# Causal attention stage: one of three products of denominator and reciprocal on GpSimd instead of VectorE

## What is computed

```python
x = x + attn_a(layernorm(x))
x = x + ffn(layernorm(x))          # two layers: local attention, then gated feed-forward
x = x + attn_b(layernorm(x))
x = x + ffn(layernorm(x))
```

```python
dot = einsum('bhid,bhjd->bhij', q, k)
vals = q_norm_sq + k_norm_sq.transpose(0, 1, 3, 2)
scores = dot * dot / (vals - 2.0 * dot + EPSILON)
attn = softmax(scores + mask)      # mask: triu(k=1) * -1e9
out = einsum('bhij,bhjd->bhid', attn, v)
```

## Time and profile before

| | us |
|---|---|
| median of 3 runs | 4480.62 |
| lowest and highest | 4475.3, 4484.98 |
| the profiled execution's span | 4472.0 |
| of that, stage b (from about 1960 to 3080) | 1120 |
| PE, DVE, ACT, POOL busy over the whole span | 93%, 74%, 57%, 37% |

### The profile page before, as it was taken

The page is one execution under the profiler, slowest core; times in us unless marked ns, Lnnn a source line. Parts: engine busy times, 40 slices in busy tenths (PEclk is TensorE's granted clock), DMA queues, the critical chain, the costliest instruction groups (busy, mean ns, idle before and its releaser), DMA issues.

```text
span 4472.0 us, 65596 instructions
## 1 busy us (share of the span) xinstructions
PE 4154.4 (93%) x23120; PEld 2610.2 (58%) x23120; DVE 3296.2 (74%) x7689; ACT 2542.1 (57%) x5480; POOL 1674.2 (37%) x1816
## 2 busy tenths in 40 slices
PE   8999989999999999988888888888999999999997
PEld 4665556666666666554555555555565665665664
DVE  5667777777667767659999999988677777677663
ACT  4555554445444445449888888876554444454441
POOL 2222355445546555330010001013464464455451
PEclk9999999999999999998888888788999999999999
DMA  2000000000000000000000001101000000100000
GB/s 78 10 16 6 24 10 5 3 3 5 23 22 18 13 8 10 23 21 18 22 20 22 20 18 28 34 20 29 9 6 3 3 25 8 30 20 17 13 19 22
DMA packets 63093, 78.57 MB, mean 18 GB/s; under 512 B 15344, under 2 KB 47392, under 8 KB 62768
## 3 DMA queue, kind: packets, MB, share of 16 engines
q1 hardware_dynamic: 62768, 74.39, 5.9%
HBM read 36.63 MB, written 12.58 MB: 11 GB/s over the span
## 4 chain that ended last, share of the span: by engine, by line
PE 64%; DVE 21%; issue 6%; ACT 5%; POOL 2%; DMA 0%; SPq 0%; POOLq 0%; DVEq 0%; ACTq 0%
PE wide L865 44%; PE o_ps L865 8%; PE wide L868 7%; PE turn_ps L868 5%; DVE x L1287 3%; DVE turned L1338 2%; DVE w_up L1387 2%; PE turn_ps L865 2%; DVE prob L1410 1%; DVE w_up L1381 1%; DVE prob L1399 1%; POOL prob L1603 1%; DVE x L1393 1%; ACT prob L1243 1%; DVE turned L1341 1%
## 5 line engine op out<-in xcount | busy, mean ns | idle before, releaser
L865 PE MATMUL wide<-x,w_up 128*128 128x512 f32 (+3 forms) x2528 | 853.8, 554 | 3.8 <-DVE x L1491 2.4
L865 PE MATMUL wide<-w_in,x_t 128*128 128x512 f32 (+2 forms) x1920 | 811.8, 567 | 17.5 <-ACT q_t L1164 8.1
L1603 POOL TENSOR_SCALAR prob<-prob,st 128x256 f32<-128x256 f32 (+1 forms) x1024 | 501.4, 508 | 775.9 <-DVE st L1423 773.6
L1223 ACT ACTIVATE prob<-prob,st 128x256 f32<-128x256 f32 (+1 forms) x1024 | 479.2, 471 | 249.1 <-DVE st L1410 248.7
L865 PEld LDWEIGHTS wide<-w_in,x_t 128*128 128x128 f32 x1920 | 341.4, 192 | 368.5 <-issue 359.6
L865 PEld LDWEIGHTS wide<-x,w_up 128*128 128x128 f32 (+2 forms) x2528 | 374.7, 198 | 288.5 <-issue 274.9
L865 PE MATMUL o_ps<-pt,v 128*32 128x128 f32 (+2 forms) x5120 | 509.3, 345 | 16.8 <-DVE pt L1439 8.6
L1576 POOL TENSOR_TENSOR sines<-raw,rot 128x512 f32<-128x512 f32 x256 | 354.0, 1403 | 331.3 <-ACT raw L1152 331.1
L865 PEld LDWEIGHTS o_ps<-pt,v 128*64 128x64 f32 (+1 forms) x5120 | 326.3, 133 | 236.6 <-issue 154.0
L1584 POOL TENSOR_TENSOR rn<-ss,minus_half 128x16 f32<-128x16 f32 x128 | 423.8, 3311 | 105.5 <-DVE ss L1333 98.7
L1254 ACT ACTIVATE o_t<-o_ps 128x512 f32<-128x512 f32 x192 | 114.2, 595 | 508.0 <-PE o_ps L865 508.0
(11 more groups left out here) (161 smaller groups left out, 7476.4 us busy)
## 6 DMA issues: line engine op xcount, KB each, us to landing
kept<-resid SPq DMA_DIRECT2D x16, 512.0 KB, 3.0
x<-kept SPq DMA_DIRECT2D x16, 512.0 KB, 3.3
w_up<-hid SPq DMA_DIRECT2D x62, 128.0 KB, 2.2
x<-hid SPq DMA_DIRECT2D x62, 128.0 KB, 2.4
shifted<-resid SPq DMA_DIRECT2D x32, 224.0 KB
w_in<-in_f_wqkv SPq DMA_DIRECT2D x4, 1536.0 KB, 6.4
w_up<-in_f_w SPq DMA_DIRECT2D x4, 1492.0 KB, 6.5
resid<-in_x SPq DMA_DIRECT2D x8, 512.0 KB, 9.0
```

What stands on the lines that cost most here:

```text
L865: return eng.matmul(out, lhsT, rhs, start=start, stop=stop, skip_group_check=True)
L1223: last = eng.activation(pr[:, local_span(t)], pr[:, local_span(t)], ACT.Exp, bias=sm[:, t:t + 1], scale=-1.0, accum_out=sm[:, 4 + t:5 + t])
L1603: last = eng.tensor_scalar(pr[:, local_span(t)], pr[:, local_span(t)], sm[:, 8 + t:9 + t], 1.0, ALU.mult, ALU.mult)
```

## The change

In steps with k % 3 == 2 the part `bclose` is replaced by a part `pclose`, which makes the same product on POOL. There are eight such steps in each of the eight units, 64 in all. The other 128 stay on DVE. `bmul` waits for whichever of the two its step has. In the planner `pclose` costs 2.5 us, where `bclose` at this width costs 0.1 + 0.277 * 4 = 1.21 us.

```diff
-        "DVE": "... bss bclip bclose bmul low inv ...",
-        "POOL": "rstd_h sin rn brow bias_b ...",
+        "POOL": "rstd_h sin rn brow pclose bias_b ...",
...
+    if kind == "pclose":
+        return 2.5
...
+def close_kind(k):
+
+    return "pclose" if k % 3 == 2 else "bclose"
...
-            put("bclose", k, at + 1 / steps, final("bguess", k))
-            put("bmul", k, at + 1.5 / steps, final("bclose", k), final("bnum", k), *scaled)
+            put(close_kind(k), k, at + 1 / steps, final("bguess", k))
+            put("bmul", k, at + 1.5 / steps, final(close_kind(k), k), final("bnum", k), *scaled)
...
-                    dve.wait_ge(S["bclose"], o)
+                    dve.wait_ge(S[close_kind(i)], nth(close_kind(i), u, i))
...
+                elif kind == "pclose":
+                    den, inv = close_home(u, i)
+                    pool.wait_ge(S["bguess"], nth("bguess", u, i))
+                    eng.tensor_tensor(den, den, inv, ALU.mult).then_inc(S["pclose"], 1)
```

More of the change, by code:

```diff
@@ L151 @@
         "DVE": "fold_o_c bn_h nrm_h cos ss join k_c ak_c row bss bclip bclose bmul low inv pt_b osum out_b res bn_f bn_f2 nrm_f xt2_c gate hid res2",
-        "POOL": "rstd_h sin rn brow bias_b wt rstd_f bias back rot pad_out pad_down pad_v",
+        "POOL": "rstd_h sin rn brow pclose bias_b wt rstd_f bias back rot pad_out pad_down pad_v",
         "SP": "load_in load_sel load_out load_rot load_up kept moved back_in store dup_a dup_b"}.items():
@@ L594 @@
         "load_fold fold_q fold_q_c fold_o fold_o_c aq aq_c lat ak_c av_c bqkv row bsq bv bss brow bk bk_c bq bq_c bias_b "
-        "score bden bdot low inv exp wt wt_b bclip bnum bln bguess bclose binv bmul turn_a turn_b neg pt_a pt_b mix sel fan out olog oexp osum out_b load_sel "
+        "score bden bdot pclose low inv exp wt wt_b bclip bnum bln bguess bclose binv bmul turn_a turn_b neg pt_a pt_b mix sel fan out olog oexp osum out_b load_sel "
         "proj res moved bn_f bn_f2 var_f rstd_f nrm_f bias xt2 xt2_c up_g gate gelu up_h hid down res2 back_in back store "
@@ L1385, in vector_program @@
                     den, inv = close_home(u, i)
-                    dve.wait_ge(S["bguess"], o)
+                    dve.wait_ge(S["bguess"], nth("bguess", u, i))
                     eng.tensor_tensor(den, den, inv, ALU.mult).then_inc(S["bclose"], 1)
```

## The result

The changed kernel is slower: 4529.59 us against 4479.25 us of the kernel before beside it, a ratio of 1.0121 (95% interval 1.0097 to 1.0145), about 54 us. The prediction was 4468 with a range of 4448 to 4498.

What follows compares the result with a forecast made beforehand. DVE, the fullest engine in stage b at 91%, was taken as the bound. 3.5 us of DVE time a unit, 28 in eight, at a half 14, less 1.5, gave 12.5 us: 4459.5 plus 8.6, 4468; range 4448 to 4498.

Steps and rivals of the forecast that it cites:

- Where the time is: Change acts in stage b, 1120 us with DVE busy 91%; the rest of the program was given nothing.
- (a): Stage b: collisions with the previous step's bmul stay as frequent; DVE 17 us longer, 4498 us; chance 0.26.
- (b): Stage b: DVE's freed time turns into waits, no change, 4479 us, between 4472 and 4489; chance 0.29.
- The price of the product: On POOL in stage b: 2.36 us each, harmless beside clips and tiles, stopping bmul for up to 2.36 us.
- The count of collisions: Stage b: 24 of 64 places collide in the old order; new order keeps two-input instructions away at six of eight steps.
- step 20: In each unit: previous step's product and bmul behind the clip, only one clip as cover; -1.2 us of DVE time.
- step 17: In each unit: long cover, bmul at some risk, collided in three units of eight; 0.2 us of DVE time gained.
- Step 2: In each unit: long cover, bmul at some risk, 0.9 us gained; the first, in unit 24, loses 1.2 us.
- The price of a collision: At one colliding place: 2.36 us of standing, less the 1.13 us freed, 1.2 us lost.
- The waits for POOL: DVE ahead of bmul: about 0.85 us with short cover, leaving 0.3 of 1.13 us freed; long cover leaves about 1.0.
- The half: Stage b: DVE has 58% of the three engines' chain; a freed microsecond worth between 0.4 and 0.6 us, half taken.
- Latency taken for covered: Between guess end and bmul: median 3.26 us over 64 steps, so a POOL product of 2.5 us fits in most.

Runs made afterwards that it cites:

- e6: Kernel before plus 48 products of 128x1024 on GpSimd in units 25 to 30, awaited by nobody, nothing taken off VectorE; ratio 1.0065.
- e10: Kernel before plus 48 times three writes of zeros on GpSimd, at the same moments as e6's products, awaited by nobody; ratio 1.0014.
- e12: Changed kernel, but GpSimd starts each product only when VectorE is done with the Newton step and maxima of the step before; ratio 1.0034.
- e5: Changed kernel with each GpSimd product cut into four instructions of 128x256, one after the other; ratio 1.0053.
- e2: Order of the kernel before on all engines, only the 64 products moved from VectorE to GpSimd; ratio 1.0104.
- e4: Changed kernel, order kept, but GpSimd multiplies only 16 elements of each row instead of 1024; ratio 0.9985.
- e9: Order of the kernel before, the 64 products off VectorE, GpSimd multiplying only 16 elements of each row; ratio 0.9955.
- e3b: Changed kernel, but in 48 of 64 steps GpSimd writes zeros of about 2.4 us instead of the product, VectorE still waiting; ratio 1.0029.
- e1: Changed kernel's order on every engine, but the 64 products made on VectorE, right ahead of the Newton step; ratio 1.0126.
- e11: Order of the kernel before, in 48 of 64 steps zeros of 2.4 us on GpSimd instead of the product, VectorE waiting; ratio 1.0048.

## Why the prediction was wrong, point by point

**Where the time is.** Right: outside stage b hardly anything moved. By the prediction's own sign (stage b longer than 1120 us) the forecast was wrong, and the signs of rivals (a) and (b) are both there: L1406 grew, and DVE's waits for POOL and PE did.

**The price of the product and the mechanism.** Right: 2.36 us forecast, 2436 ns measured; it is harmless beside clips and tiles and stops the maxima. e6 against e10, e12 and e5 show it three times. The Trainium skill's rule on the shared port pair ("SBUF — State Buffer", section "SBUF: two separate sides") holds here also in its finer point, that a GpSimd instruction which reads no SBUF does not block an instruction with two SBUF inputs: 595 ns in e10.

**The count of collisions.** Wrong: the sum had step 20 in every unit and step 17 in three, eleven in all. There were 18 with a row maximum. Step 20 was one, as named, in six units. Step 2, which the sum put among the gainers with "some risk", was the other: it collided in five units of eight. I had judged it by its cover and not by where the previous bmul stood. The new order was counted to have far fewer collisions than the 24 of the old one; on the chip the old order had 16 (e2), so it did not have fewer. And `bias_b` beside L1400 was in no count.

**The price of a collision.** On VectorE's own account right: the sum charged 2.36 us of standing, and 2.69 - 0.55 = 2.1 us were measured. The waits for POOL are right too: 0.1 to 0.8 us at each of seven steps were charged, 20 us in all, and 22.6 measured. With 18 collisions, 38 us, the account would be 72 - 38 - 23 = 11 us to the good, against 28 forecast. But by its busy time VectorE gained only 18 us, and 18 - 23 leaves nothing. By the sum's own way of counting that makes the time the same as before, not 54 us longer.

**The half.** This is the step that failed most: "A microsecond freed on DVE is therefore worth between 0.4 and 0.6 us", which the sum applied to the relief, the waits and the blocking alike. In us of kernel time:

| term of the sum | at a half | measured |
|---|---|---|
| 72 us off VectorE | -36 | -7 in the new order (e4), -20 in the old (e9) |
| waits for POOL, 20 us | +10 | +20, with 16 products in it (e3b against e4) |
| blocking (2.3 us a unit at step 20, 0.7 at step 17), 24 us | +12 | +41 in 48 of the 64 steps (changed against e3b) |
| together | -14 | +54 |

The half was read from the chain of before, which shows who held the stage at its load of then. Measured, a microsecond of VectorE had no one price. Taken out of the order that was dealt with the products in it, 72 us gave 20, about 0.3 each, and the chain went to PE and ACT. In the order dealt without them, the same products cost 63 us (e1 against e4), 0.8 each, and that order with the products on VectorE is 56 us slower than the kernel before (e1); the 7 us of e4 are what is left of both. The blocking of 48 steps cost 41 us where it took 27 us of standing from the maxima (126 x 0.21); in e6 it was less than its standing, 29 us for 38 us on the two groups shown. Rival (b) had the waits and rival (a) the collisions; both came at once, and the range had been built as if only one could hold. Rival (a) had the sign right and named the mechanism, but at 17 us for VectorE and 4498 for the kernel it was too cheap by the same step.

**Latency taken for covered.** The median of 3.26 us between guess and bmul was read as room for 2.5 us. But in that time DVE did its own product; with it out, DVE is there earlier and waits, and what it feeds waits with it. The size of these waits was charged rightly; what they cost the kernel, up to 20 us in the new order (e3b against e4), was charged at half.

**The sum that fits.** In us from the ratios, at 4475 us each: VectorE relieved, in the new order -7; latency, with 16 products left, +20; blocking in 48 steps +41; together 54, which is the 1.2% measured. It has to close, since these are steps of one ladder; what supports it is that e12, another way to take the blocking away, gives the same 0.9%. That the blocking costs 41 us in this order and 25 us in the old one (e2 against e11) is a difference within the noise of the four runs.

**Left open.** Why the blocking cost more than its standing here and less in e6, and why the price of VectorE's time depends so much on the order. PE's busy time over the span rose from 4154 to 4179 us with the same instructions, and the granted clock in stage b was 0.82 or 0.83 against 0.84; in e2 it was 0.81. Longer gaps on PE and a lower clock go together in these rows, but no run here set one alone. A lower clock is not needed for a loss, though: e1 lost 56 us with the clock of stage b at 0.85. Between executions of the kernel before itself time and clock also move together: 4448.44 us at a mean granted clock of 0.965 and 4485.58 us at 0.950. How ScalarE and TensorE share stage b with VectorE relieved is settled only as far as the chain shows it.

## What to carry to other kernels

Ask of a two-input product on GpSimd not only whether its time is covered, but which VectorE instructions run beside it: with two SBUF inputs they stand for up to its whole length (2.69 us for 0.55 us of work). If it must be there, start it behind them (one wait gave 0.9%) or cut it into pieces (0.7%). And when three engines are above 80% busy, don't turn freed time into kernel time by one factor, neither by the share in the chain of waits nor by how far the fullest engine stands above the next: VectorE stood 76 us above ScalarE in stage b, 72 us were taken off it, and the gain was 20 us. A run with the work simply left out (e9) measures that factor before anything is moved.

## What the runs showed that I had not expected

An added wait made the kernel faster by 0.9% (e12), and four short instructions on GpSimd were better than one long one although they took longer together (252 pieces of 0.72 to 0.73 us mostly, some 2.8 us for four):

```profile
2517.88 2.79 POOL L1610 TENSOR_TENSOR w_up<-w_up,hid 128x256 f32<-128x256 f32 x4
```

A product that nobody waits for and that replaces nothing on VectorE cost 0.6 us of kernel time (e6), 0.5 us more than zeros at the same moments (e10).
